# LSTM pick: the semaphores of score, maximum and pick return to zero in each step, and their waits compare with the constant 1

## The reference, cut to what matters

```python
def step(carry, x_t):
    h, c = carry
    sel_in = jnp.concatenate([h, c, x_t], axis=-1)
    logits = sel_in @ W_sel.T + b_sel                                # 4 scores
    onehot = jax.nn.one_hot(jnp.argmax(logits, axis=-1), Sx)         # the pick
    g_all = einsum('bi,sgi->bsg', x_t, W_ih) + einsum('bh,sgh->bsg', h, W_hh) + b_ih + b_hh
    g = jnp.einsum('bsg,bs->bg', g_all, onehot)                      # 2048 gates of the picked cell
    i, f, g, o = split(g, 4); c = sigmoid(f) * c + sigmoid(i) * tanh(g); h = sigmoid(o) * tanh(c)
```

## Time and profile before

| | |
|---|---|
| runs (3), median | 6420.35 us |
| profiled execution | 6423.3 us |
| its span | 6421.3 us |
| TensorE busy | 5387.0 us (84%) |
| VectorE busy | 3158.5 us (49%) |
| granted TensorE clock, mean | 0.945 |
| steps of the LSTM (first to last MAX8) | 2306.9 to 5677.7 us |

### The profile page before, as it was taken

One profiled execution on the slowest core, in us unless ns is written; L12 is line 12 of the kernel. 1 busy time (PEld: TensorE's weight loads), 2 busy tenths in 40 slices (PEclk: granted clock), 3 DMA queues, 4 the chain that ended last, 5 costly groups with the idle time before them and its releaser, 6 DMA issues. The chain is left out here.

```text
span 6421.3 us, 214665 instructions
## 1 busy us (share of the span) xinstructions
PE 5387.0 (84%) x84946; PEld 3259.0 (51%) x84948; DVE 3158.5 (49%) x13265; ACT 1088.2 (17%) x4645; POOL 613.4 (10%) x1014
## 2 busy tenths in 40 slices
PE   8997878849989658888888888888888888878778
PEld 6543443324657435555555555555555555544444
DVE  4402443214541365555555555555555555555543
ACT  0000000012321131111111111111111111122312
POOL 0000750003630000000000000000000000001100
PEclk9998989979999879999999999999999999989877
DMA  0000111566433400000000000000000000000010
GB/s 10 26 26 10 40 41 39 120 173 209 120 97 130 182 16 5 10 5 5 5 5 10 5 5 5 5 5 10 5 5 5 5 10 0 0 23 36 14 62 8
DMA packets 128787, 240.28 MB, mean 37 GB/s; under 512 B 47084, under 2 KB 64114, under 8 KB 127687
## 3 DMA queue, kind: packets, MB, share of 16 engines
q1 hardware_dynamic: 68584, 146.72, 6.5%
q0 software_dynamic: 60128, 92.58, 5.7%
HBM read 165.58 MB, written 73.29 MB: 37 GB/s over the span
## 5 line engine op out<-in xcount | busy, mean ns | idle before, releaser
L1457 PE MATMUL bank<-lstm_w,step_h_parts 128*32 128x128 f16 (+1 forms) x59904 | 1229.7, 237 | 327.8 <-issue 327.8
L1457 PEld LDWEIGHTS bank<-lstm_w,step_h_parts 128*32 128x32 f16 x59904 | 1109.1, 97 | 648.4 <-issue 634.5
L1427 PE MATMUL bank<-lstm_w 128*128 128x512 f16 x4992 | 1296.7, 382 | 3.3 <-issue 3.3
L1481 DVE TRANSPOSE_TENSOR_REDUCE step_summed<-bank 128x4 f32<-128x128 f32 x1872 | 670.6, 358 | 299.5 <-PE bank L1457 278.9
L1427 PEld LDWEIGHTS bank<-lstm_w 128*128 128x128 f16 x4992 | 386.3, 98 | 388.8 <-issue 5.1
L1406 ACT ACTIVATE step_act_out<-step_gates 128x4 f32<-128x4 f32 x625 | 128.6, 206 | 2124.2 <-DVE step_gates L1487 2120.8
L1534 DVE COPY step_xgs<-step_xg 128x16 f32 x624 | 109.0, 175 | 731.1 <-issue 705.3
L1487 DVE SCALAR_TENSOR_TENSOR step_gates<-step_summed,lstm_inv_scale,step_xgs 128x4 f32<-128x4 f32 x1872 | 414.9, 222 | 64.8
L1396 POOL COPY xnT<-step_state 128x4 f32 (+1 forms) x625 | 116.5, 186 | 3317.3 <-DVE step_state L1514 3317.3
L1109 PE MATMUL bank<-sum_parts,sum_hot 125*125 125x512 f16 x1600 | 347.6, 381 | 6.7 <-DVE sum_parts L1068 6.7
L1437 PE MATMUL bank<-lstm_wsel,step_state 128*1 128x4 f32 x4992 | 214.9, 168 | 110.7 <-DVE step_state L1504 110.7
(11 more groups left out here) (368 smaller groups left out, 6617.4 us busy)
## 6 DMA issues: line engine op xcount, KB each, us to landing
rel_h<-rel_h_sb SPq DMA_DIRECT2D x39, 1024.0 KB, 4.3
lstm_xg<-xg_g POOLq DMA_DIRECT2D x4, 5000.0 KB, 19.5
step_xg<-lstm_xg SPq DMA_DIRECT2D x25, 800.0 KB, 4.4
xg_w<-in_c_w_ih SPq DMA_DIRECT2D x8, 2048.0 KB, 10.8
lstm_w<-in_c_w_hh SPq DMA_DIRECT2D x4, 4096.0 KB, 31.0
rel_z<-rel_z_sb POOLq DMA_DIRECT2D x8, 1250.0 KB, 22.9
rel_zg<-rel_z POOLq DMA_DIRECT2D x8, 1248.0 KB
cheb_w<-in_L_gnn_weight SPq DMA_DIRECT2D x8, 1024.0 KB
```

The costliest lines, as they stand in the source:

```text
L1427: nc.tensor.matmul(idle[:], w[:, 0, 0, 0, 0, 0:128], w[:, 0, 0, 0, 0, :], start=True, stop=True)
L1457: last = nc.tensor.matmul(bank[32 * q:32 * q + 32, 0:32 * (end - first)], h_parts[:, c, :], w[:, s, c, q, a, 32 * first:32 * end], start=( ...
L1481: nc.vector.tensor_reduce(summed[:, first:end], bank[:, 0:32 * (end - first)].rearrange("p (b r) -> p b r", r=32), X_AXIS, ALU.add, apply_ ...
```

## The change

Three semaphores of the pick, `score_done`, `top_ready` and `picked`, no longer count the steps. Each is raised by one as before and is lowered by one again by VectorE's sequencer in the same step: `score_done` and `top_ready` behind the copy of the input part, `picked` behind the first row sum of the next `finish`. Their waits compare with the constant 1, and the waits for `init` beside them go.

```diff
@@ TensorE, in the loop over t @@
                 keep_clock_up(1)
-                pe.wait_ge(init, 1)
-                pe.wait_ge(picked, t)
+                pe.wait_ge(picked, 1)
                 s = pe.value_load(pick[0:1, 0:1])
@@ VectorE @@
             def choose(t):
-                dve.wait_ge(init, 1)
-                dve.wait_ge(score_done, t)
+                dve.wait_ge(score_done, 1)
                 nc.vector.max(top[:], score).then_inc(top_ready, 1)
-                dve.wait_ge(init, 1)
-                dve.wait_ge(top_ready, t)
+                dve.wait_ge(top_ready, 1)
                 nc.vector.max_index(pick[:], top[:], score).then_inc(picked, 1)
-                dve.wait_ge(init, 1)
-                dve.wait_ge(picked, t)
+                dve.wait_ge(picked, 1)
                 s = dve.value_load(pick[0:1, 0:1], min_val=0, max_val=CELLS - 1)
                 dve.wait_ge(xg_loaded, (t // CHUNK + 1) * 16)
                 nc.vector.tensor_copy(xgs[:], xg[:, bass.ds(s, 1), bass.ds((t % RING) * GC, GC)]
                                       ).then_inc(xgs_ready, 1)
+                dve.sem_inc(score_done, -1)
+                dve.sem_inc(top_ready, -1)

             def finish(t, n):
                 add_rows(part_f, t)
+                dve.sem_inc(picked, -1)
                 dve.wait_ge(xgs_ready, t)
                 add_input(part_f, t)
```

## The result

The changed kernel takes 6273.42 us (median of 4 runs, 6271.63 to 6278.15), the kernel before 6421.31 in the same comparison: 147.9 us less, ratio 0.9771 (95% interval 0.9754 to 0.9788). The prediction was 6275, range 6255 to 6314. The profiled execution took 6278.15 us, its span 6276.3, which is 145.0 less than in the earlier trace rows.

The account below looks back on a forecast made before the run. The pick's serial chain, then TensorE from the cell on, was taken to bound each turn; 0.06 + 0.068 + 0.105 = 0.233 us over 624 turns gave 145 us less, 6275 us, range 6255 to 6314.

Parts of the forecast that it names:

- What bounds the turn: One chain through the pick, with no second engine beside it, then TensorE from the cell on; 5.41 us a turn.
- MATCH_VALUE_LOAD, 0.068: Gap between MAX8's end and MATCH_VALUE_LOAD falls from 0.103 to 0.035 us, saving 0.068 a turn; bounds 0.05 and 0.08.
- The rival that the waits stay instructions of their own: At the pick's waits: still sequencer instructions though they compare with a constant; time within 0.2%, 6420 us; 2 in 100.
- MAX8, 0.06, bounds 0 and 0.07: Wait between the last score product and MAX8: saves 0.06 us a turn, nothing if L1519 already holds MAX8, at most 0.07.
- The rival of the engine's drain: MAX8 and MATCH_VALUE_LOAD start when VectorE lets them; only TensorE's 0.105 a turn stays, 66 us, 6355; 4 in 100.
- TensorE's load, 0.105: Between FIND_INDEX8's end and the cell's first product, one instruction (0.051 us) and one hand-over (0.054) go; bounds 0.05, 0.12.
- The rival that TensorE's sequencer is held until its fourth idle product leaves the queue: TensorE's register load can't start before 3501.87, so only 0.10 a turn is kept, 62 us, 6358; 6 in 100.
- The lowerings: Three on VectorE's sequencer, 0.07 us each; two behind the copy make the sum of f late by 0.16, hidden.
- The sum: Over a turn 0.06 + 0.068 + 0.105 = 0.233 us, 624 turns: 145 us saved, all on the chain.
- The slower rival: Between copy and sum of f: lowerings over 0.25 us make VectorE's sequencer the bound; at 0.35, 6545; 3 in 100.

## Why the prediction was right, point by point

- **What bounds the turn.** Right. Every part moved the total by its own gap, 624 times; all of the gain is inside the loop.
- **MATCH_VALUE_LOAD, 0.068.** Right: 0.103 to 0.034 in the trace, 39.8 us alone (0.064 a turn). The rival that the waits stay instructions of their own is out.
- **MAX8, 0.06, bounds 0 and 0.07.** Slightly under: 0.071 in the trace, 42.3 us alone (0.068). The two limits that I weighed, the score and the engine behind L1519, lie within 0.01 of each other: MAX8 is 0.04 behind the one and 0.085 behind the other. Where L1519 was made late, this second limit set the time. The rival of the engine's drain is out.
- **TensorE's load, 0.105.** Right as worked out from durations and hand-overs (a wait of 51 ns and 54 ns behind it in the turn of the earlier trace rows): the load starts 0.039 behind FIND_INDEX8, 0.150 before, which is 0.111; alone 66.4 us (0.106 a turn). The rival that TensorE's sequencer is held until its fourth idle product leaves the queue is out: the load now starts 0.087 ahead of that product (0.083 at the least, 621 turns).
- **The lowerings.** The mechanism was right, the size was off: 0.10 each, not 0.07. So the sum of f is 0.57 behind the copy, not 0.53. In most turns it stays hidden, with 0.10 (median) instead of 0.14 to spare; in those of the earlier trace rows, where I had 0.03 to spare, it is not: they won 0.221 instead of 0.242, 4 us over 195 turns.
- **The sum.** 145 forecast, 147.9 measured. The parts by trace are 0.250 a turn (0.071 + 0.068 + 0.111), 156 us. The late f takes 4; the rest, 0.008 a turn, I have not settled. In the 428 turns the trace has 0.006 of it between the cell's first product and the sum of i and g (mean), and the rest in hand-overs that became a few ns longer. So the forecast came within 2 us of the time in part by luck: two terms taken low by 11 us together, against some 9 us of losses that the sum did not have. The lower end of the range, 6255, is not what the upper bounds give either, 6252.
- **The slower rival.** Its mechanism is real, with its place: two lowerings more cost 63 us. Its point, 0.25 us for a lowering, was never near.

What failed were above all two expectations behind the prediction. That a lowering behind weigh_h is free assumed that the sequencer runs ahead of an engine instruction whose wait is on the instruction; here it does not. And that the new c is not late read the 0.163 between sigmoid and tanh as ScalarE's pace, when it was the tanh's wait for c.

## What to carry to other kernels

At i times g and the new c this brought 75.9 us on top of the changed kernel and asks for no lowering; the waits for `init` in the loop look like the same case, untested. Where no wait can be dropped, see whether one can be moved to an instruction that has time. What is added in exchange belongs where the sequencer is neither about to hand over what is late nor behind an instruction that waits; and two starts that look like an engine's pace can be two waits that end together, so set each apart before it is called hidden.

## What the runs showed of the hardware

- A wait that is the sequencer's own instruction puts VectorE's instruction 0.103 behind the end of what it waits for, one on the instruction 0.034. For TensorE's register load it is 0.150 and 0.039, for VectorE's 0.107 and 0.039.
- A semaphore lowering by VectorE's sequencer shows 21 ns in its record and costs 0.095 to 0.10 us of the sequencer's time; two in a row 0.19.
- It doesn't overtake an instruction that still waits: behind the sum of f the lowering starts 0.024 us after the sum's own start (0.007 at the least), behind weigh_h 0.014 after, though both instructions carry their wait themselves. The register addition behind the sum of i and g (L1492 of before) starts 0.014 after it in all 623 turns. The lowering of `picked` leans on this order: the sum of f waits for the cell, so TensorE has long seen `picked` at 1 when it falls. The Trainium skill ("Perfetto Trace Analysis", "DVE / Act Engine Instruction (TENSOR_ADD, Activation, etc)") has the sequencer free for the next instruction once the waiting one is in the wait queue. For an instruction of the sequencer itself these runs show otherwise: moved behind weigh_h, two lowerings cost 37.4 us. Behind the sum of o, whose wait had ended, the first one ran ahead of the sum's start, by 0.129 us (median).
- VectorE can start a maximum 0.082 us behind the start of a tensor_tensor of 0.177 us, before that one's end, when the maximum's own wait has already ended (the kernel with the lowerings behind weigh_h).
